# Whitening 32 images: weights folded into the last product, bias a phase later, norm later, product crossed, stores issued by SyncE

## What is computed

```python
x1 = x.reshape(N, C // G, G, H, W).transpose(0, 2, 1, 3, 4).reshape(N, G, -1)   # N=32, C=256, G=32, H=W=48
mean = x1.mean(-1, keepdims=True)
xc = x1 - mean
cov = xc @ xc.transpose(0, 2, 1) / M + EPS * jnp.eye(G)
decorr = isqrt_newton_schulz(cov, 10)
# Y = A/|A|, Z = I; ten times: T = 0.5*(3I - Z@Y); Y = Y@T; Z = T@Z; result Z/sqrt(|A|)
y = weight1 @ decorr @ xc + bias1
return y.reshape(N, G, C // G, H, W).transpose(0, 2, 1, 3, 4).reshape(N, C, H, W)
```

## Time and profile before

| | us |
|---|---|
| median of 3 runs | 467.77 (463.84 to 476.04) |
| the profiled execution | 462.93 |
| its span, first to last instruction | 461.0 |

### The profile page before, as it was taken

One profiled execution on the slowest core, in us unless ns is written; L12 is line 12 of the kernel. 1 busy time (PEld: TensorE's weight loads), 2 busy tenths in 40 slices (PEclk: granted clock), 3 DMA queues, 4 the chain that ended last, 5 costly groups with the idle time before them and its releaser, 6 DMA issues.

```text
span 461.0 us, 17013 instructions
## 1 busy us (share of the span) xinstructions
PE 379.3 (82%) x7392; PEld 271.3 (59%) x7392; DVE 329.4 (71%) x1033; ACT 332.9 (72%) x450; POOL 56.8 (12%) x108
## 2 busy tenths in 40 slices
PE   0868899898989899898989897989999897977700
PEld 0856766666657667675756665666767575633100
DVE  5767887797869777988868787779888786643000
ACT  5772478797969868787878787787878796455800
POOL 0000001111111111020111111111102011112500
PEclk9976999999999989999989999899999999999965
DMA  7999939999999999999999999999999666677990
GB/s 271 416 409 410 412 141 284 338 346 351 381 358 404 357 394 344 398 390 390 385 383 362 381 394 382 367 327 388 384 391 388 218 208 208 200 213 225 312 268 18
DMA packets 28747, 152.11 MB, mean 330 GB/s; under 512 B 3968, under 2 KB 3968, under 8 KB 20736
## 3 DMA queue, kind: packets, MB, share of 16 engines
q0 software_dynamic: 9952, 75.50, 46.6%
q1 hardware_dynamic: 18432, 75.51, 43.2%
q10 hardware_dynamic: 288, 0.01, 0.0%
HBM read 75.51 MB, written 75.50 MB: 328 GB/s over the span
## 4 chain that ended last, share of the span: by engine, by line
PE 67%; DVE 11%; ACT 8%; issue 5%; DMA 2%; POOL 1%; SPq 0%; DVEq 0%; POOLq 0%; ACTq 0%
PE cov_ps L432 29%; PE y_ps L493 25%; PE chain_ps L464 6%; ACT image L220 6%; DVE transposed L315 5%; PE chain_ps L462 2%; DMA image<-x 2%; PE cov_ps L444 1%; PE chain_ps L474 1%; POOL y L188 1%; DVE yz L353 1%; DVE t_mat L354 1%; DVE col L350 1%; ACT image L230 1%; PE chain_ps L466 1%
## 5 line engine op out<-in xcount | busy, mean ns | idle before, releaser
L315 DVE STREAM_TRANSPOSE transposed<-image 128x384 f32<-128x384 f32 x384 | 215.7, 572 | 13.5 <-ACT image L220 2.8
L230 ACT ACTIVATE image<-y_ps,y_bias 128x768 f32<-128x768 f32 x192 | 164.8, 894 | 68.4 <-PE y_ps L493 67.7
L432 PE MATMUL cov_ps<-transposed 128*64 128x65 f32 x4608 | 178.7, 231 | 5.4 <-issue 5.4
L493 PE MATMUL y_ps<-image,apply_w 64*64 64x384 f32 x1536 | 171.8, 513 | 4.4 <-issue 2.3
L432 PEld LDWEIGHTS cov_ps<-transposed 128*64 128x64 f32 x4608 | 160.9, 142 | 14.5 <-issue 6.3
L220 ACT ACTIVATE image<-image,shift 128x1152 f32<-128x1152 f32 x128 | 156.1, 1248 | 1.8 <-DMA image<-x 0.8
L493 PEld LDWEIGHTS y_ps<-image,apply_w 64*64 64x64 f32 x1536 | 58.9, 135 | 15.1 <-ACT image L230 7.6
L186 POOL DMA_DIRECT2D y<-image x34 | 19.4, 572 | 381.1 <-ACT image L230 381.1
L462 PEld LDWEIGHTS chain_ps<-yz 128*64 128x64 f32 (+1 forms) x288 | 32.8, 138 | 35.4 <-DVE yz L367 27.3
L367 DVE SCALAR_TENSOR_TENSOR yz<-yz,chain_ps 64x96 f32<-64x96 f32 x144 | 33.8, 234 | 22.9 <-PE chain_ps L464 16.9
L464 PE MATMUL chain_ps<-yz,t_mat 64*64 64x96 f32 x256 | 47.0, 265 | 3.4 <-DVE t_mat L362 3.4
(11 more groups left out here) (59 smaller groups left out, 167.1 us busy)
## 6 DMA issues: line engine op xcount, KB each, us to landing
image<-x SPq DMA_DIRECT2D x128, 576.0 KB, 11.2
y<-image POOLq DMA_DIRECT2D x31, 1152.0 KB, 8.6
y<-image POOLq DMA_DIRECT2D x62, 576.0 KB, 11.0
y<-image POOLq DMA_DIRECT2D x3, 384.0 KB, 12.2
y<-image POOLq DMA_DIRECT2D x6, 192.0 KB, 11.6
b_col<-bias ACTq DMA_DIRECT2D x4, 0.1 KB, 6.3
w_nat<-weight ACTq DMA_DIRECT2D x2, 4.0 KB, 4.3
```

Of the source, the lines that this page charges most:

```text
L230: nc.scalar.activation(xs[n % SLOTS][:, :, STRIP * q:STRIP * (q + 1)], y_ps[:, f % 2, :, 0:STRIP], ACT.Identity, bias=y_bias[:, c % 2, i:i ...
L315: nc.vector.transpose(xt[q][:, TILES // 2 * part:TILES // 2 * (part + 1), 0:CH], xs[n % SLOTS][:, h, at:at + TWELFTH]).then_inc(transposed, 1)
L432: ins = nc.tensor.matmul(cov_ps[rows, n % 2, 0:GRAM], xt[q][:, t, 0:CH], xt[q][:, t, 0:GRAM], start=q == 0 and t < 2, stop=q == IMAGE_PIEC ...
L493: ins = nc.tensor.matmul(y_ps[out_rows, f % 2, h, 0:STRIP], apply_w[rows, c % 2, i].rearrange("p k g -> p (k g)"), xs[n % SLOTS][rows, h, ...
```

## The change

What it does:

- The tenth Newton step isn't carried out on Z alone: in the step LAST one matmul forms both Z x Y (for the last T) and Z x W^T; VectorE makes `t_wide` and `folded` from it, and SPREAD is one product of the two for each output half (2 matmuls for 6). The chain has two steps less.
- The chain's offset (the mean's share of the bias) is computed a turn later, from `apply_w` and `means`, by four one-column matmuls in slot 0 and one VectorE instruction; ScalarE's output 0 waits for its semaphore `offset_dve`, and so does the NORM matmul of the next pair. `gather` gets one more matmul and GATHER one more copy; `d_mask` goes.
- NORM's matmul moves from slot 1 to slot 2, its vector part from slot 1 to slot 4, and NEXT_0 from slot 3 to slot 5. ScalarE's `root` moves behind output 0, and `half_root` a round later.
- The output product puts its two row groups into the two banks of `y_ps` and reads half 0 and half 1 for the two halves of the output rows, so that channel 128 o + 64 r + p lies in partition 64 o + p at r.
- An image is stored by two DMAs of 128 partitions (in DRAM 2 blocks of 64 rows), issued by SyncE; its loads are interleaved: store n, then the load of image n + 9.

```diff
+LAST = NEXT_0 + 1 + 2 * (NEWTON - 2)
+SPREAD = LAST + 1
+OFFSET_AT, NORM_AT, NORM_OUT_AT, NEXT_0_AT = 0, 2, 4, 5
+PE_AT = {NORM_AT: NORM} | {NEXT_0_AT + t - NEXT_0: t for t in range(NEXT_0, SPREAD + 1)}
+DVE_AT = {NORM_OUT_AT: NORM} | {NEXT_0_AT + t - NEXT_0: t for t in range(NEXT_0, SPREAD + 1)}
...
-    out_v = out.rearrange("n (h p) a b -> n p h (a b)", h=HALVES)
+    out_v = out.rearrange("n (o r p) a b -> n r o p (a b)", o=HALVES, r=2)
...
+            def store(n, pieces):
+                sp.wait_ge(y_read, IMAGE_PIECES * n + pieces.stop)
+                cols = slice(STRIP * pieces.start, STRIP * pieces.stop)
+                for r in range(2):
+                    sp.dma_start(out_v[n, r, :, :, cols], xs[n % SLOTS][:, r, cols]).then_inc(stored[n % SLOTS][r], 16)
+            for n in range(SLOTS):
+                load(n)
+            for n in range(IMAGES):
...
+                    store(n, slice(0, IMAGE_PIECES))
+                if 0 < n and n - 1 + SLOTS < IMAGES:
+                    load(n - 1 + SLOTS)
...
-                pool.dma_start(out_v[n, :, 0, cols], slot[:, 0, cols]).then_inc(stored[n % SLOTS][0], 16)
-                for rows, channels in ((slice(0, HALF), slice(HALF, P)), (slice(HALF, P), slice(0, HALF))):
-                    pool.dma_start(out_v[n, channels, 1, cols], slot[rows, 1, cols]).then_inc(stored[n % SLOTS][1], 16)
...
+                    if exists(c - 2):
+                        output(c - 2, 2 * j)
                     if j == 0 and exists(c - 1):
                         root(c - 1)
-                    if exists(c - 2):
-                        output(c - 2, 2 * j)
...
+                elif t == LAST:
+                    weighted, product = product, chain_ps[0:Q, C_PRODUCT + G:C_PRODUCT + 2 * G]
+                    link(nc.vector.scalar_tensor_tensor(
+                        out=t_wide[:], in0=product.unsqueeze(1).to_broadcast([Q, 2, G]), scalar=-0.5, in1=eye15_wide[:],
+                        op0=ALU.mult, op1=ALU.add))
+                    link(nc.vector.scalar_tensor_tensor(
+                        out=folded[:], in0=weighted.unsqueeze(1).to_broadcast([Q, PAIR, G]), scalar=RSQ, in1=own,
+                        op0=ALU.mult, op1=ALU.mult))
...
+            def offset(c):
+                pe.wait_ge(chain_dve, OPS_TOTAL * (c + 1))
+                for half in range(2):
+                    for i in range(PAIR):
+                        ins = nc.tensor.matmul(chain_ps[HALF * half:HALF * (half + 1), C_OFFSET + i:C_OFFSET + i + 1],
+                                               apply_w[:, c % 2, i].rearrange("p k g -> p (k g)"),
+                                               means[:, c % 2, i:i + 1], start=True, stop=True)
+                ins.then_inc(offset_pe, 1)
...
-                        h = row ^ half
-                        ins = nc.tensor.matmul(y_ps[out_rows, f % 2, h, 0:STRIP], apply_w[rows, c % 2, i].rearrange("p k g -> p (k g)"),
-                                               xs[n % SLOTS][rows, h, STRIP * q:STRIP * (q + 1)], start=True, stop=True)
+                        ins = nc.tensor.matmul(y_ps[out_rows, f % 2, row, 0:STRIP],
+                                               apply_w[rows, c % 2, i].rearrange("p k g -> p (k g)"),
+                                               xs[n % SLOTS][rows, half, STRIP * q:STRIP * (q + 1)],
+                                               start=True, stop=True)
```

More of the change, by code:

```diff
@@ L51 @@
 GATHER, NORM, NEXT_0 = 0, 1, 2
[L52 to L55, removed]
+LAST = NEXT_0 + 1 + 2 * (NEWTON - 2)
[3 more added lines that the diff above has]
+DVE_AT = {NORM_OUT_AT: NORM} | {NEXT_0_AT + t - NEXT_0: t for t in range(NEXT_0, SPREAD + 1)}
+assert max(PE_AT) == ROUNDS * SLOTS_A_ROUND - 1
 ASIDE = NEXT_0 + 8
-EXTRA = {t: 1 for t in range(ASIDE, ASIDE + 4)} | {NORM: 1}
-OPS = {t: 1 + EXTRA.get(t, 0) for t in range(NORM, SPREAD + 1)} | {GATHER: 4, NORM: 6, SPREAD: 2}
+EXTRA = {t: 1 for t in range(ASIDE, ASIDE + 3)} | {GATHER: 1, NORM: 1}
+OPS = {t: 1 + EXTRA.get(t, 0) for t in range(NORM, SPREAD + 1)} | {GATHER: 5, NORM: 6, LAST: 2}
 OPS_TOTAL = sum(OPS.values())
 STEPS = SPREAD + 1
-C_COV, C_REST, C_OUTER = 0, G, G + 4
-C_NORM, C_PRODUCT, C_NEXT, C_SPREAD, C_OFFSET = 0, 0, G, 2 * Q, 0
+C_COV, C_REST, C_MEANS, C_OUTER = 0, G, G + 2, G + 4
+C_NORM, C_PRODUCT, C_NEXT, C_SPREAD, C_OFFSET = 0, 0, Q, 3 * Q, 4 * Q
 YZ = G + Q
@@ L150, in whiten @@
         chain_act = sem("chain_act")
+        offset_pe = sem("offset_pe")
+        offset_dve = sem("offset_dve")
         y_done = sem("y_done")
@@ L164, in _, with load @@
         def _(sp):
-            for n in range(IMAGES):
+            def load(n):
                 for p in range(QUARTERS):
@@ L291, in _ @@
             dve.wait_ge(shift_mat_ready, 1)
-            for zeros in (yz, t_mat, parity):
+            for zeros in (wyz, t_mat, parity, means):
                 then(nc.vector.memset(zeros[:], 0.0))
@@ L302, in _ @@
             then(nc.vector.tensor_scalar(eye15[:], eye[0:Q, 0:Q], 1.5, None, ALU.mult))
[L303 to L304 removed]
+            then(nc.vector.tensor_scalar(eye15_wide[:], eye_col[0:Q, :].unsqueeze(1).to_broadcast([Q, 2, G]), 1.5, None,
+                                         ALU.mult))
+            then(nc.vector.tensor_scalar(mean_mat[:], eye_col[:].unsqueeze(1).to_broadcast([P, 2, G]), 1.0 / SAMPLES,
+                                         None, ALU.mult))
             def transpose(n, k):
@@ L360, in chain @@
                                                         op0=ALU.mult, op1=ALU.add))
-                elif t < FOLD and (t - NEXT_0) % 2 == 1:
+                elif t < LAST and (t - NEXT_0) % 2 == 1:
                     link(nc.vector.scalar_tensor_tensor(
@@ L364, in chain @@
                         op0=ALU.mult, op1=ALU.mult))
[L365 to L371, removed]
+                elif t < LAST:
+                    link(nc.vector.scalar_tensor_tensor(out=yz[0:Q], in0=yz[0:Q], scalar=1.5, in1=following,
+                                                        op0=ALU.mult, op1=ALU.add))
[3 more added lines that the diff above has]
+                        out=t_wide[:], in0=product.unsqueeze(1).to_broadcast([Q, 2, G]), scalar=-0.5, in1=eye15_wide[:],
+                        op0=ALU.mult, op1=ALU.add))
+                    link(nc.vector.scalar_tensor_tensor(
+                        out=folded[:], in0=weighted.unsqueeze(1).to_broadcast([Q, PAIR, G]), scalar=RSQ, in1=own,
+                        op0=ALU.mult, op1=ALU.mult))
                 else:
@@ L398, in _ @@
                     j = s // SLOTS_A_ROUND
-                    if s in STEP_AT and exists(c - 1):
-                        chain(c - 1, STEP_AT[s])
+                    if s == OFFSET_AT and exists(c - 2):
+                        offset(c - 2)
+                    if s in DVE_AT and exists(c - 1):
+                        chain(c - 1, DVE_AT[s])
                     if s == 9 and exists(c):
@@ L479, in chain, with offset @@
-                ins.then_inc(chain_pe, 1)
+                        ins = nc.tensor.matmul(chain_ps[HALF * half:HALF * (half + 1), C_SPREAD:C_SPREAD + PAIR * G],
+                                               t_wide[:].rearrange("p k g -> p (k g)"),
+                                               folded[:].rearrange("p i g -> p (i g)"), start=True, stop=True)
+                ins.then_inc(chain_pe, 1)
+            def offset(c):
+                pe.wait_ge(chain_dve, OPS_TOTAL * (c + 1))
[5 more added lines that the diff above has]
+                ins.then_inc(offset_pe, 1)
@@ L506, in _ @@
                         covariance(PAIR * c + 2 * j // IMAGE_PIECES, 2 * j % IMAGE_PIECES)
-                    if s in STEP_AT and exists(c - 1):
-                        chain(c - 1, STEP_AT[s], slice(0, P) if exists(c) else slice(0, Q))
+                    if s == OFFSET_AT and exists(c - 2):
+                        offset(c - 2)
+                    if s in PE_AT and exists(c - 1):
+                        chain(c - 1, PE_AT[s], slice(0, P) if exists(c) else slice(0, Q))
                     ahead = PAIR * c + 1 + j // 3
```

85 lines of the change are left out of this document (38 added, 47 removed).

## The result

| | us |
|---|---|
| the changed kernel, median of 4 runs | 1603.78 (1600.84 to 1604.67) |
| the kernel before beside it, median of 4 | 467.82 (463.84 to 476.04) |
| ratio | 3.437 (3.415 to 3.459) |
| span of the profiled execution | 1599.0 |

The prediction said 425 us. The kernel became 3.4 times slower. It is rival A, priced at 1640, that came.

A forecast was written before the change was run, and what follows sets the result against it. TensorE, with a 1.66 us hole before NEXT_0, was taken to set the beat, with the DMA keeping up. From span 461.0, -20.5 - 1.5 - 7.5 - 8.3 = -37.8 gave 423, time 425 us; range 410 to 1680.

The forecast's parts named there:

- rival A: Two-block stores dealt by outermost count to two of 16 DMA engines: 1640 us; chance 0.42.
- Stores of 128 partitions: Stores at the end go at 380 GB/s, last landing 7 us after the last output instead of 15: -7.5 us.
- Stores by SyncE: Stores issued by SyncE: GpSimd's DRAIN goes, -8.3 us; SyncE's order of loads and stores costs 0, bound +8.
- Share 0.15: Sign of rival A: a DMA share of about 0.15.
- Stores above 20 us: Sign of rival A: stores take over 20 us to land.
- Eight engines would make 34 us a pair: In rival A's pricing: stores on eight engines would give 34 us a pair; it decides below 14 engines.
- Norm later, chain shorter: TensorE's wait before NEXT_0 0.7 us for 1.66, less chain work: 1.5 us a pair, beat 22.9, -20.5 us in all.
- Crossing 0: Output product with each bank written by one row group: 0 us, bounds -19 and +19 us.
- DRAIN -8.3: GpSimd's DRAIN of 8.40 us at the block's end goes with its DMAs: -8.3 us, bounds 0 and -8.4.
- SyncE's order 0, bound +8: Loads queued behind stores on SyncE go out up to 12 us late, paid by a 24 us lead: cost 0, bound +8.
- B (446): The beat stays at 24.3 us, held by ScalarE or DMA; only the end gains, -17: 446 us; chance 0.08.
- C (458): Little comes: GpSimd's drain stays 8.4, landing as slow, SyncE's order costs 8: 458 us; chance 0.04.

The follow-up runs named there:

- Experiments 1 and 2: Changed kernel with each store cut at the block boundary: 433.44 us; with its stores' DRAM side walked as 16, 8 or 4 blocks: 435.02, 584.4, 907.5 us.
- cut at 64 rows: Changed kernel with each store cut at the block boundary, four DMAs of 64 rows an image, issued by SyncE: 433.44 us, run again 436.72 us.
- kernel with 16 blocks: Changed kernel with the stores' DRAM side walked as 16 blocks of 8 rows instead of 2 of 64, 128 partitions kept: 435.02 us.
- crossed kernel: Changed kernel with its crossed output product, stores cut into four DMAs of 64 rows: 436.72 us issued by SyncE, 458.20 us issued by GpSimd.
- SyncE alone: Kernel before with its stores issued by SyncE in the changed kernel's order, nothing else changed: 457.27 us, ratio 0.983.

## Why the prediction was wrong

The forecast was a gain, and the kernel got slower. The stated range of 410 to 1680 us did reach the result, but only because it had been stretched to rival A.

**The step that failed** is "*Stores of 128 partitions*", and in it the assumption of the likeliest case that a DMA of 2 x 64 rows against 128 is dealt over all engines like one of 128. It went by the hardware queue's shapes so far, "the trace has no DMA with unequal lists", and gave 0.46 to it and 0.42 to A. Experiments 1 and 2 show what holds in its place: the outermost DRAM count, two, is the number of engines, and the same two for each of SyncE's stores (packets in progress, above). A pair takes 99.7 us where 22.9 was expected. *Stores by SyncE*, put down at a cost of 0 to 8 us, has its part in it: the same stores issued by GpSimd make 583 us and not 1604. The rule of the Trainium skill cited there (DMA: Bandwidth & Descriptors, "Why a DMA increments its semaphore by 16 and not by 1") spoke against the change; the packet counts agree with it in all walks, and no row of before spoke for the even dealing, which got the larger chance.

**Rival A, term by term.** 130 packets a store: 130. Share 0.15: 0.13 with stores alone, but 0.27 with loads beside them and 0.25 over the span, so this sign was put too low. Stores above 20 us: the trace gives no landing for them; their issue alone lasts 15.5 us in the median. ScalarE waits for loads: 824 us. The price of 1640 for 1604 is off mainly by one term, an engine's speed: I took 25.8 GB/s from the loads' mean of 412 and it moved 26.7 to 27.0. With 27.0 the same sum is 82.0 MB / 54 GB/s + 69 = 1587, 12 us less than the span of 1599. "Eight engines would make 34 us a pair": 35.1 in the row.

**The rest of the forecast**, which the cut at 64 rows lets one read:

- *Norm later, chain shorter.* 1.5 us a pair expected, beat 22.9. Undisturbed pairs take 23.1 to 23.4 in every kernel with the new chain: a gain of 1.2 us. The wait of the NEXT_0 matmul was said to be 0.7 for 1.66; in the first run of cut at 64 rows the list of waits and the timeline have:

```profile
PE chain_ps L489 <- DVE t_mat L370: 9.7, 12, 1.2
```
```profile
228.70 0.24 PE L489 MATMUL chain_ps<-wyz,t_mat 64*64 64x32 f32 x1 [0.89 <-DVE t_mat L370]
```

  Twelve waits of 0.81 on average, for 1.5 (20.7 over 14). The mechanism was right, the size a quarter too large. But alone the chain gives 12 us (2.6%), not 20.5: with it TensorE has stalls of "issue" in several pairs, 18.5 us in all for 7.9 before, in one execution each. I had not counted on these waits for instructions.
- *Crossing 0.* Together with the pieces some 6 us of gain with SyncE's stores and none with GpSimd's, inside my bounds of 19. No run has the crossed product as its only difference.
- *Stores of 128 partitions, -7.5 at the tail.* Too large by itself too. The tail in the kernel with 16 blocks, whose stores have 128 partitions and all engines, and in cut at 64 rows:

```profile
419.10:431.40 12.30, 0.00 (x0) 0.00 (x0) 0.00 (x0) 0.00 (x0) 0.00 (x0) 0.59 0.77 276
```
```profile
418.70:432.90 14.20, 0.00 (x0) 0.00 (x0) 0.00 (x0) 0.03 (x1) 0.00 (x0) 0.60 0.82 267
```

  I had put down 224 and 270 GB/s to 64 partitions and expected 380. With 128 the mean is 276, and the end comes 12.3 us after the last output, not 7; -1.9 us against 64 rows, about -3 against before's 15.5, in one execution each. The tail of the 16-block kernel in four pieces shows where the 380 went:

```profile
419.10:422.00 2.90, 0.00 (x0) 0.00 (x0) 0.00 (x0) 0.00 (x0) 0.00 (x0) 0.86 1.03 388
422.00:426.00 4.00, 0.00 (x0) 0.00 (x0) 0.00 (x0) 0.00 (x0) 0.00 (x0) 0.50 0.96 329
426.00:429.00 3.00, 0.00 (x0) 0.00 (x0) 0.00 (x0) 0.00 (x0) 0.00 (x0) 0.50 0.84 295
429.00:431.40 2.40, 0.00 (x0) 0.00 (x0) 0.00 (x0) 0.00 (x0) 0.00 (x0) 0.50 0.07 28
```

  The rate of 380 is there while all engines are busy, but only for 3 us: the engines run out one after the other, and 2.4 us at the end move next to nothing. The sum had the whole tail at the full rate.
- *DRAIN -8.3.* Right: 8.396 us gone, and back in the kernel that stores by GpSimd again. With the crossed kernel's pieces it is 3.8 us, so its length isn't fixed, and what sets it is open.
- *SyncE's order 0, bound +8.* With SyncE alone the last output came 4.5 us later than before in one execution each, less than executions differ. In the crossed kernel SyncE's stores let it come 12 us earlier. The order costs nothing that shows, and with the new chain the move gained more than the drain.

So the forecast's 425 failed by the dealing. Without that it would still have been too low, by the tail and by the stalls: it stood for a saving of 8.2% (425 for 462.93), and the kernel that cuts at 64 rows saves 7.2 and 5.8%. The parts as measured, 12 for the chain, 3 for the tail and 8.3 for the drain, add up to 23 of its 27 to 34 us; the rest isn't told apart. That kernel beats the one before and the changed one. Rivals B (446) and C (458) were not what happened either: the beat fell, and the drain went. That rival A's price came within 3% was no luck, since its terms hold one by one; the error was to give the even dealing the larger chance.

## What to carry to other kernels

Before a DMA's pattern is reshaped, look at the outermost count of its DRAM side, which was varied here, and not only at the number of partitions: the change made a store look wider (128 partitions for 64) and it ran on 2 engines of 16. Packets give it away at once, since rows and closings add up to 130 for 144, and so does a DMA share that stays at 2/16 while stores are waiting. Where both kinds of traffic share a queue order, stores on few engines hold up the loads too. And where a case rests wholly on a thing that the trace can't show, a rule that speaks of it should set the forecast, and the price of being wrong (1200 us against 40) should be looked at before the chance.

A gap of TensorE that waits for nothing in the list of waits may be a wait for its instructions. Compare its end with the packets of the instruction queue before looking for a cause in the kernel's order.

## What the hardware showed that was not expected

- The issuing engine changes which engines a narrow DMA gets: the same 68 two-block stores took the kernel to 583 us from GpSimd and to 1604 from SyncE. The software queue had 67,648 packets for 75.75 MB there, 61,664 of all packets under 512 B, for 9,952. Its rows weren't cut up: 7,936 packets of 9,216 B are in both traces, and 59,328 of the others have 4 or 8 bytes, 0.25 MB in all. What they are for is open.
- Stores alone at a share of 1.03 moved 388 GB/s (16 blocks, above), loads alone move 412. Over a whole tail the mean is 276 with 128 partitions and 267 with 64, since the engines run out.
- TensorE's waits for instructions at full DMA share last up to 3.7 us in the first run of cut at 64 rows, and the clock falls behind some. The timeline of TensorE and a stretch of cut at 64 rows:

```profile
202.84 1.38 PE L457 MATMUL cov_ps<-transposed 128*64 128x65 f32 x24 [3.67 <-issue]
```
```profile
203.10:206.50 3.40, 3.40 (x50) 2.45 (x48) 0.76 (x2) 0.00 (x0) 0.00 (x0) 0.50 0.99 405
```

  The pair with this stall took 27.8 us for 23.2: 3.67 of stall, and the rest goes with a granted clock of 0.50, the lower level. Their sum differs between two executions of the same kernel (12.3 and 15.5 us), which is a part of why the last outputs differ (418.7 and 425.5).
